# Cross-attention kernel: the two image chunks' picks in one matmul that opens the transposed scores, key turns behind the last weighted values, score turns behind a projection

## The chip, the cores and the metric

The kernel runs on one core of a Trainium2 chip. The metric is the device time of one execution in microseconds (us); the kernel before takes 1612.66 us, the median of three runs (1612.31 to 1616.88). Five engines work side by side, each through its own queue: TensorE (PE for matmuls, PEld for the loads of their weights), VectorE (DVE), ScalarE (ACT), GpSimd (POOL) and SyncE (SP, which issues DMAs). They wait for each other through semaphores.

## The reference

For each of 32 batches there are 112 tokens and a context of 375 rows (257 image rows, 118 text rows), 512 wide. The first layer is cross-attention with 16 heads of 32:

```
q = rms_norm(linear(layernorm(x), q_w, q_b), norm_q_w)
k, k_img = rms_norm(linear(ctx_txt, ...)), rms_norm(linear(ctx_img, ...))
out = softmax(q k_img^T / sqrt(32)) v_img + softmax(q k^T / sqrt(32)) v
x = x + linear(out, o_w, o_b)
```

The second layer picks 14 of the 112 tokens of each batch by a router score, runs a transformer block (causal attention over all 448 picked tokens, gated MLP) on them and adds the result to the layer norm of x, which is added to x.

## The kernel before, in words

The first 165 us project all queries. Then a loop goes over the batches: `body(i, n, m, p)` for batches 0 to 30 (i is this batch, n = i + 1 the one whose keys and values are projected meanwhile, m = i + 2, p = i - 1 the one that is finished), and `last` for batch 31. From 1240 us on comes the second layer. The order on every engine is written out by hand: each engine has its own `body`, and semaphores tie them.

PE's `body`, in its order. `scores(i, g)` for the four groups g of four heads gives scores by query, of which DVE takes each row's top (`group_max`). Between them stand projections: `values`, `output`, `keys`, each four to twelve matmuls of 512 columns in full shape (128 rows by 128 columns of weights). `turn_top` transposes the tops. `scores_T(i, g)` makes the scores again, by key, for four heads at once, one head in each 32-row strip of the array: three chunks of keys (119 text rows with an image row, and 128 and 128 image rows). In each chunk four matmuls multiply keys and queries in float32, which the trace shows as two records each, and four more (the picks, L1533) subtract the tops, in fp32r, one record each. The chunks lie side by side in a PSUM bank per head: columns 0 to 111, 112 to 223, 224 to 335. All four banks are read by ACT's `exps(i, g)` (L774 for the text chunk, L776 for both image chunks), and the next `scores_T` waits for that. `weighted_values(i, g, n)` (L1555) multiplies the probabilities by the values in 32-column strips, six sources of four matmuls (eight records) each; the last source is `prob_img`, for the image softmax's sum. POOL makes `prob_img` in `sum_image(i, g)` (L532) out of ACT's two image chunks, DVE adds the text chunk's image row to it in `add_tail(i, g)` (L1075), and only then can that last source start. DVE's `normalise(i, g)` (L1081, L1083, L1087) reads what comes out. `turn(n, k)` (L1477) transposes the three key tiles that DVE has scaled (`add_bias` L1049, `scale_k` L1055), and ACT's `split_kq` (L756 to L763) copies them out for the next batch's scores. It then copies a value tile (`value_image`, L785). `turn_score(p)` (L1515) transposes batch p's router score, whose ranks DVE counts.

POOL's `body` also splits the context (L495), takes roots (`inverse_rms`, L526), adds for the output (`output`, L536) and adds a bias row to the next residual (`residual`, L540, 112x512). ACT's and DVE's orders are not touched.

Of the kernel before, what the change touches and what calls it, by code (L numbers as in the profile page):

```python
# [12 lines left out]
B, L, D = 32, 112, 512  # L13
IMG, CTX = 257, 375
TXT = CTX - IMG
NH, HD = 16, 32
P = 128
KC = D // P
GH = P // HD
# [4 lines left out]
CHUNK_C = TXT + 1  # L24
# [7 lines left out]
CHUNKS = [(0, CHUNK_C), (CHUNK_C, P), (CHUNK_C + P, P)]  # L32
# [18 lines left out]
def build(nc, t, out):  # L51
    with ExitStack() as ctx:
# [3 lines left out]
        def sem(name):  # L56
            return ctx.enter_context(nc.semaphore(name))

        ps = ctx.enter_context(nc.psum_tensor("ps", [P, 8, 512], F32))
# [49 lines left out]
        pick_c = p1("pick_c", [P, NG, CHUNK_C], F32R)  # L109
        pick_img = p1("pick_img", [P, NG, P], F32R)  # L110
# [21 lines left out]
        k_all = p1("k_all", [P, KC, NKEY])  # L132
        q_hi = p1("q_hi", [P, NG, L], F32R)
        q_all = p1("q_all", [P, NG, L])
# [26 lines left out]
        topT = [p1(f"topT{e}", [P, L], F32R) for e in range(2)]  # L161
# [122 lines left out]
        st_full, exp_done, img_summed, tail_added = sem("st_full"), sem("exp_done"), sem("img_summed"), sem("tail_added")  # L284
# [206 lines left out]
        def _(pool):  # L491
# [36 lines left out]
            def sum_image(i, g):  # L528
                pool.wait_ge(exp_done, 8 * i + 2 * g + 2)
                if not isinstance(i, int) or i or g >= 2:  # L530
                    pool.wait_ge(pv_full, 4 * i + g - 1)
                nc.gpsimd.tensor_tensor(prob_img[:, g % 2], prob[:, g % 2, 1, :], prob[:, g % 2, 2, :], ALU.add).then_inc(img_summed, 1)  # L532
# [68 lines left out]
            def body(i, n, m, p):  # L601
                split_ctx(n)
                if p is not None:
                    normalise_h(p)
                inverse_rms(n, 1)
                if p is not None:
                    output(p)
                sum_image(i, 0)
                inverse_rms(n, 2)
                sum_image(i, 1)  # L610
                inverse_rms(n, 3)
                sum_image(i, 2)
                if p is None:
                    pool.wait_ge(rows_ready, 2)
                residual(i)
                sum_image(i, 3)

            def gather(c):
                nc.gpsimd.indirect_dma_start(xh_sel[:, c].rearrange("l a d -> l (a d)"), None, xh_dram[0:EARLY_B * L] if c < EARLY else xh_dram,
# [802 lines left out]
        def _(pe):  # L1422
# [89 lines left out]
            def turn_score(p):  # L1512

                pe.wait_ge(score_ready, p + 1)
                nc.tensor.transpose(ps[0:L, 7, 2 * L:3 * L], score_now[:].to_broadcast([L, L]), ident[0:L, 0:L]).then_inc(score_turned, 1)  # L1515

            def scores_T(i, g):
                if g == 0:
                    pe.wait_ge(s_done, 4 * i + 4)
                else:  # L1520
                    pe.wait_ge(exp_done, 8 * i + 2 * g)
                if g % 2 == 0:
                    pe.wait_ge(topT_ready, 2 * i + 1 + g // 2)
                for c, (at, rows) in enumerate(CHUNKS):
                    cols = slice(at, at + rows)
                    out_cols = slice(c * L, (c + 1) * L)
                    pick = pick_c if c == 0 else pick_img
                    for j in range(GH):
                        head = slice(HD * j, HD * (j + 1))
                        nc.tensor.matmul(ps[0:rows, 2 + j, out_cols], k_all[head, g, cols], q_all[head, g, :], start=True, stop=False)  # L1530
                    for j in range(GH):
                        head = slice(HD * j, HD * (j + 1))
                        last = nc.tensor.matmul(ps[0:rows, 2 + j, out_cols], pick[head, g, :], topT[g // 2][head, :], start=False, stop=True)  # L1533
                last.then_inc(st_full, 1)

            def weighted_values(i, g, n):
                pe.wait_ge(exp_done, 8 * i + 2 * g + 2)
                if g == 0:
                    pe.wait_ge(vtail_loaded, 16 * i + 16)
                    pe.wait_ge(b0_done, 4 * i + 4)  # L1540
                    pe.wait_ge(b1_done, value_slot(i, 1)[3] + 1)
                if g >= 2:
                    pe.wait_ge(pv_done, 4 * i + g - 1)
                bank = 6 + g % 2
                p_c, p_a, p_b = (prob[:, g % 2, c, :] for c in range(3))
                sources = ((0, ((v_last, p_c, CHUNK_C), (v_a, p_a, P), (v_b, p_b, P))), (1, ((v_txt, p_c, CHUNK_C),)),
                           (3, ((ones_txt, p_c, CHUNK_C),)), (2, ((ones_all, prob_img[:, g % 2], P),)))
                for slot, terms in sources:
                    for e, (left, right, rows) in enumerate(terms):
                        if slot == 2:  # L1550
                            pe.wait_ge(tail_added, 4 * i + g + 1)
                        for j in range(GH):
                            h = GH * g + j
                            cols = slice(HD * h, HD * (h + 1)) if slot < 2 else slice(0, HD)
                            last = nc.tensor.matmul(ps[HD * j:HD * (j + 1), bank, slot * L:(slot + 1) * L], left[0:rows, cols],  # L1555
                                                    right[0:rows, L * j:L * (j + 1)], start=e == 0, stop=e == len(terms) - 1)
                last.then_inc(pv_full, 1)
# [37 lines left out]
            def body(i, n, m, p):  # L1595
                scores(i, 0)
                values(i, 2)
                scores(i, 1)
                if p is not None:
                    output(p)  # L1600
                scores(i, 2)
                if p is not None:
                    pe.wait_ge(pv_done, 4 * i)
                turn_top(i, 0)
                keys(n, 0)
                scores(i, 3)
                keys(n, 1)
                turn_top(i, 1)
                scores_T(i, 0)
                keys(n, 2)  # L1610
                scores_T(i, 1)
                if p is not None:
                    pe.wait_ge(topT_ready, 2 * i + 2)
                    turn_score(p)
                weighted_values(i, 0, n)
                values(n, 0, range(0, 2))
                scores_T(i, 2)
                if p is not None:
                    pe.wait_ge(rank_done, i)
                weighted_values(i, 1, n)  # L1620
                scores_T(i, 3)
                values(n, 0, range(2, 4))
                weighted_values(i, 2, n)
                pe.wait_ge(exp_done, 8 * i + 8)
                for k in range(1, 4):
                    turn(n, k)
                weighted_values(i, 3, n)
                values(n, 1)

            hot = slot_hot[:].rearrange("l b k -> l (b k)")  # L1630
# [86 lines left out]
            for kc in range(KC):  # L1717
                made = nc.tensor.transpose(ps[:, kc // 2, L * (kc % 2):L * (kc % 2 + 1)], normed_last[:, kc * P:(kc + 1) * P], ident[0:L, 0:L])
# [174 lines left out]
```

## Time and profile before

| | us |
|---|---|
| median of three runs | 1612.66 |
| the profiled execution | 1612.68 |
| its span, first to last instruction | 1610.7 |
| PE busy | 1560.9 |
| PEld busy | 1213.2 |
| DVE busy | 1201.0 |
| ACT busy | 708.5 |
| POOL busy | 706.6 |

The loop over the batches has one pattern that repeats itself each 34.2 us. A timeline of one pass (here the one in which `scores_T(i, 0)` starts at 780.55 us) therefore stands for 31. In a timeline each row has the start, the duration, the engine, the line, the operation, what it writes and reads, and in brackets how long the engine stood idle before it and what ended that. Matmuls are pipelined: the distance from one start to the next is what a matmul costs, its duration is its latency.

### The profile page before, as it was taken

The numbers are of one execution on the slowest core, as the hardware profiler recorded it, in microseconds if no ns is written. First come the engines' busy times: TensorE is split into PE (matmuls) and PEld (weight loads), VectorE is DVE, ScalarE is ACT, GpSimd is POOL, SyncE is SP. The second block draws the span as 40 slices with busy tenths as digits, with TensorE's granted clock in tenths as the row PEclk, the third lists the DMA queues.
The fourth block names the chain that finished last, engine by engine and source line by source line (L and its number), as shares of the span: only waits on it lengthen the run. The fifth ranks groups of instructions, "written<-read, shape, count | busy, mean of one in ns | idle before, by whom it ended". The sixth has DMA issues, their size and how long they took to land.

```text
span 1610.7 us, 42276 instructions
## 1 busy us (share of the span) xinstructions
PE 1560.9 (97%) x16758; PEld 1213.2 (75%) x16758; DVE 1201.0 (75%) x1887; ACT 708.5 (44%) x1458; POOL 706.6 (44%) x785
## 2 busy tenths in 40 slices
PE   7999999999999999999999999999997999999997
PEld 5776777777777777777777777777776786777997
DVE  5753778877788878788788788787887586553986
ACT  5763444443444443444444444434444223555431
POOL 6762344334434344444344443344343592113752
PEclk9999999999999999999999999999997999999999
DMA  6842121112211112211112111122116324001000
GB/s 194 245 134 60 56 61 52 49 48 67 67 51 53 48 48 72 65 48 53 48 51 75 59 53 48 48 67 69 49 35 237 123 104 158 27 27 53 1 1 23
DMA packets 66167, 113.71 MB, mean 71 GB/s; under 512 B 21392, under 2 KB 36080, under 8 KB 64576
## 3 DMA queue, kind: packets, MB, share of 16 engines
q1 hardware_dynamic: 65280, 110.20, 21.5%
q0 software_dynamic: 832, 2.75, 0.6%
q8 instruction: 37, 0.61, 0.2%
q14 instruction: 18, 0.15, 0.0%
HBM read 82.59 MB, written 30.34 MB: 70 GB/s over the span
## 4 chain that ended last, share of the span: by engine, by line
PE 90%; ACT 5%; DVE 2%; POOL 1%; issue 1%; DMA 0%; ACTq 0%; POOLq 0%; DVEq 0%; SPq 0%
PE ps L1425 22%; PE ps L1426 19%; PE ps L1427 19%; PE ps L1555 8%; PE ps L1530 7%; PE ps L1503 3%; PE ps L1477 3%; PE ps L1759 2%; PE ps L1742 2%; ACT prob L776 2%; PE ps L1533 2%; PE ps L1751 1%; PE ps L1459 1%; ACT prob L774 1%; PE ps L1510 1%
## 5 line engine op out<-in xcount | busy, mean ns | idle before, releaser
L495 POOL TENSOR_TENSOR ctx_lo<-ctx_raw,ctx_hi 128x472 fp32r<-128x472 f32 x64 | 115.2, 1821 | 310.5 <-ACT ctx_hi L717 310.5
L532 POOL TENSOR_TENSOR prob_img<-prob 128x448 f32<-128x448 f32 x128 | 160.1, 1251 | 190.1 <-ACT prob L776 190.1
L1081 DVE RECIPROCAL rec<-ps 128x224 f32<-128x224 f32 x128 | 199.0, 1555 | 6.1 <-PE ps L1555 2.5
L774 ACT ACTIVATE prob<-ps 119x448 f32<-119x448 f32 x128 | 69.8, 545 | 210.6 <-PE ps L1533 210.6
L1530 PEld LDWEIGHTS ps<-q_all,k_all 32*128 32x128 f32 (+1 forms) x3072 | 121.9, 187 | 45.7 <-issue 31.8
L1070 DVE TENSOR_REDUCE top<-ps 112x4 f32<-112x1028 f32 x128 | 156.3, 1221 | 0.0
L1530 PE MATMUL ps<-q_all,k_all 32*128 32x112 f32 (+1 forms) x3072 | 148.3, 301 | 6.2 <-ACT prob L776 6.2
L750 ACT ACTIVATE sq_junk<-proj 128x513 bf16<-128x513 f32 (+1 forms) x96 | 61.2, 637 | 172.5 <-DVE proj L1049 172.5
L1069 DVE TENSOR_REDUCE top<-ps 112x4 f32<-112x472 f32 x128 | 83.0, 649 | 66.0 <-PE ps L1503 66.0
L1075 DVE SCALAR_TENSOR_TENSOR prob_img<-prob,ones_last,prob_img 23x448 f32<-23x448 f32 x128 | 90.3, 706 | 38.5 <-POOL prob_img L532 35.5
L776 ACT ACTIVATE prob<-ps 128x896 f32<-128x896 f32 x128 | 117.0, 914 | 0.0
L1425 PE MATMUL ps<-w_v_img_hi,ctx_hi 128*128 128x512 f32 x256 | 110.7, 433 | 0.0
L1425 PE MATMUL ps<-w_k_img_hi,ctx_hi 128*128 128x512 f32 x256 | 107.6, 420 | 0.0
L1427 PE MATMUL ps<-w_v_img_hi,ctx_lo 128*128 128x512 f32 x256 | 101.0, 395 | 0.0
L1426 PE MATMUL ps<-w_v_img_lo,ctx_hi 128*128 128x512 f32 x256 | 100.9, 394 | 0.0
L1427 PE MATMUL ps<-w_k_img_hi,ctx_lo 128*128 128x512 f32 x256 | 100.7, 393 | 0.0
L1426 PE MATMUL ps<-w_k_img_lo,ctx_hi 128*128 128x512 f32 x256 | 100.7, 393 | 0.0
L1049 DVE TENSOR_TENSOR proj<-ps,ki_bias 128x512 f32<-128x512 f32 x64 | 44.3, 693 | 50.6 <-PE ps L1427 50.6
L1427 PE MATMUL ps<-hT_hi,ring_lo 128*128 128x448 f32 x224 | 82.0, 366 | 0.0
L1533 PE MATMUL ps<-topT,pick_img 32*128 32x112 f32 x1024 | 81.3, 297 | 0.0
L526 POOL TENSOR_TENSOR rstd<-sq_sum,neg_half 128x1 f32<-128x1 f32 x96 | 52.7, 549 | 56.2 <-ACT sq_junk L750 56.2
L1338 DVE TENSOR_REDUCE neg_top<-ps 112x1 f32<-112x112 f32 (+1 forms) x64 | 28.5, 446 | 58.3 <-PE ps L1743 58.2
(333 smaller groups left out, 4416.7 us busy)
## 6 DMA issues: line engine op xcount, KB each, us to landing
ctx_raw<-in_ctx_dram SPq DMA_DIRECT2D x32, 748.0 KB, 4.2
xh_dram<-xh SPq DMA_DIRECT2D x32, 448.0 KB, 3.1
q_dram<-q_turned SPq DMA_DIRECT2D x28, 256.0 KB, 2.8
q_all<-q_dram SPq DMA_DIRECT2D x32, 224.0 KB, 3.0
xh<-in_x_dram SPq DMA_DIRECT2D x32, 224.0 KB, 2.8
out_dram<-out_sb SPq DMA_DIRECT2D x32, 224.0 KB, 2.3
xa<-in_x_dram SPq DMA_DIRECT2D x21, 256.0 KB, 3.4
ring<-in_wq_dram SPq DMA_DIRECT2D x1, 4096.0 KB, 13.9
```

The lines of the kernel that those rows point to most:

```text
L495: nc.gpsimd.tensor_tensor(ctx_lo[:, :, cols], ctx_raw[:, :, cols], ctx_hi[:, :, cols].bitcast(F32), ALU.subtract).then_inc(ctx_lo_done, 1)
L532: nc.gpsimd.tensor_tensor(prob_img[:, g % 2], prob[:, g % 2, 1, :], prob[:, g % 2, 2, :], ALU.add).then_inc(img_summed, 1)
L776: nc.scalar.activation(prob[:, g % 2, 1:3, :].rearrange("p c (j q) -> p j c q", j=GH), ps[:, 2:6, L:3 * L].rearrange("p j (c q) -> p j c q ...
L1070: nc.vector.tensor_reduce(rows[:, :, 2 * g + 1], ps[0:L, 2:6, TAIL:CTX], AX.X, ALU.max).then_inc(s_done, 1)
L1075: nc.vector.scalar_tensor_tensor(prob_img[last_rows, g % 2], prob[last_rows, g % 2, 0, :], ones_last[last_rows, 0:1], prob_img[last_rows, ...
L1081: nc.vector.reciprocal(rec[:], bank[:, 2:4]).then_inc(norm_step, 1)
L1425: nc.tensor.matmul(o_, a_hi, b_hi, start=start, stop=False)
L1426: nc.tensor.matmul(o_, a_hi, b_lo, start=False, stop=False)
L1427: return nc.tensor.matmul(o_, a_lo, b_hi, start=False, stop=stop)
L1530: nc.tensor.matmul(ps[0:rows, 2 + j, out_cols], k_all[head, g, cols], q_all[head, g, :], start=True, stop=False)
L1533: last = nc.tensor.matmul(ps[0:rows, 2 + j, out_cols], pick[head, g, :], topT[g // 2][head, :], start=False, stop=True)
L1555: last = nc.tensor.matmul(ps[HD * j:HD * (j + 1), bank, slot * L:(slot + 1) * L], left[0:rows, cols], right[0:rows, L * j:L * (j + 1)], st ...
```

## The change

On PE, `scores_T` now opens each chunk's sum with the pick instead of closing it, and the picks of the two image chunks, which have the same weights and the same moving operand, become one matmul of 224 columns that reads `topT` twice by a step of zero. In PE's `body`, `turn_score(p)` stands ahead of `scores_T(i, 1)` and so directly behind the projection `keys(n, 2)`; `weighted_values(i, 3, n)` stands ahead of the three key turns, directly behind `weighted_values(i, 2, n)`. Its own wait takes the place of the explicit one. On POOL, `sum_image(i, 3)` stands ahead of `residual(i)`. PE's `last` keeps its order; only its `scores_T` change.

```
--- before
+++ after
@@ POOL body
                 sum_image(i, 2)
+                sum_image(i, 3)
                 if p is None:
                     pool.wait_ge(rows_ready, 2)
                 residual(i)
-                sum_image(i, 3)
@@ scores_T
-                for c, (at, rows) in enumerate(CHUNKS):
-                    cols = slice(at, at + rows)
-                    out_cols = slice(c * L, (c + 1) * L)
-                    pick = pick_c if c == 0 else pick_img
+                def products(c, stop):
+                    at, rows = CHUNKS[c]
                     for j in range(GH):
                         head = slice(HD * j, HD * (j + 1))
-                        nc.tensor.matmul(ps[0:rows, 2 + j, out_cols], k_all[head, g, cols], q_all[head, g, :], start=True, stop=False)
-                    for j in range(GH):
-                        head = slice(HD * j, HD * (j + 1))
-                        last = nc.tensor.matmul(ps[0:rows, 2 + j, out_cols], pick[head, g, :], topT[g // 2][head, :], start=False, stop=True)
-                last.then_inc(st_full, 1)
+                        made = nc.tensor.matmul(ps[0:rows, 2 + j, c * L:(c + 1) * L], k_all[head, g, at:at + rows], q_all[head, g, :],
+                                                start=False, stop=stop)
+                    return made
+
+                for j in range(GH):
+                    head = slice(HD * j, HD * (j + 1))
+                    nc.tensor.matmul(ps[0:CHUNK_C, 2 + j, 0:L], pick_c[head, g, :], topT[g // 2][head, :], start=True, stop=False)
+                products(0, True)
+                for j in range(GH):
+                    head = slice(HD * j, HD * (j + 1))
+                    nc.tensor.matmul(ps[:, 2 + j, L:3 * L].rearrange("p (c q) -> p c q", c=2), pick_img[head, g, :],
+                                     topT[g // 2][head, :].unsqueeze(1).to_broadcast([HD, 2, L]), start=True, stop=False)
+                products(1, False)
+                products(2, True).then_inc(st_full, 1)
@@ PE body
                 keys(n, 2)
-                scores_T(i, 1)
                 if p is not None:
                     pe.wait_ge(topT_ready, 2 * i + 2)
                     turn_score(p)
+                scores_T(i, 1)
                 weighted_values(i, 0, n)
@@ PE body
                 weighted_values(i, 2, n)
-                pe.wait_ge(exp_done, 8 * i + 8)
+                weighted_values(i, 3, n)
                 for k in range(1, 4):
                     turn(n, k)
-                weighted_values(i, 3, n)
                 values(n, 1)
```

PE, one pass of the loop, from `scores_T(i, 1)` on, before. L1530 are products, L1533 picks, L1515 is the score turn, L1555 the first source of `weighted_values(i, 0, n)`:

```order
L1530 MATMUL ps<-q_all,k_all 119x112 x4
L1533 MATMUL ps<-topT,pick_c 119x112 x4
L1530 MATMUL ps<-q_all,k_all 128x112 x4
L1533 MATMUL ps<-topT,pick_img 128x112 x4
L1530 MATMUL ps<-q_all,k_all 128x112 x4
L1533 MATMUL ps<-topT,pick_img 128x112 x4
L1515 MATMUL ps<-ident,score_now 112x112
L1555 MATMUL ps<-prob,v_last 32x112 x4
```

The same place after; L1528 are products, L1534 and L1538 picks, L1562 `weighted_values`:

```order
L1515 MATMUL ps<-ident,score_now 112x112
L1534 MATMUL ps<-topT,pick_c 119x112 x4
L1528 MATMUL ps<-q_all,k_all 119x112 x4
L1538 MATMUL ps<-topT,pick_img 128x224 x4
L1528 MATMUL ps<-q_all,k_all 128x112 x8
L1562 MATMUL ps<-prob,v_last 32x112 x4
```

The score turn has moved ahead, the picks open the sums, and one four of picks of 112 columns is gone where another has become 224 wide.

PE at the end of the pass, from the last source of `weighted_values(i, 2, n)` to the first matmul of `values(n, 1)`, before; L1477 are the key turns:

```order
L1555 MATMUL ps<-prob_img,ones_all 32x112 x4
L1477 MATMUL ps<-ident,proj 128x118 x4
L1477 MATMUL ps<-ident,proj 128x128 x8
L1555 MATMUL ps<-prob,v_last 32x112 x4
L1555 MATMUL ps<-prob,v_a 32x112 x4
L1555 MATMUL ps<-prob,v_b 32x112 x4
L1555 MATMUL ps<-prob,v_txt 32x112 x4
L1555 MATMUL ps<-prob,ones_txt 32x112 x4
L1555 MATMUL ps<-prob_img,ones_all 32x112 x4
L1425 MATMUL ps<-w_v_img_hi,ctx_hi 128x512
```

and after:

```order
L1562 MATMUL ps<-prob_img,ones_all 32x112 x4
L1562 MATMUL ps<-prob,v_last 32x112 x4
L1562 MATMUL ps<-prob,v_a 32x112 x4
L1562 MATMUL ps<-prob,v_b 32x112 x4
L1562 MATMUL ps<-prob,v_txt 32x112 x4
L1562 MATMUL ps<-prob,ones_txt 32x112 x4
L1562 MATMUL ps<-prob_img,ones_all 32x112 x4
L1477 MATMUL ps<-ident,proj 128x118 x4
L1477 MATMUL ps<-ident,proj 128x128 x8
L1425 MATMUL ps<-w_v_img_hi,ctx_hi 128x512
```

The twelve turns have moved behind the six sources of the last group, which now has nothing between it and the group before.

POOL from the first sum of a pass to its last instruction, before; L532 is `sum_image`, L526 a root, L540 `residual`:

```order
L532 TENSOR_TENSOR prob_img<-prob 128x448
L526 TENSOR_TENSOR rstd<-sq_sum,neg_half 128x1
L532 TENSOR_TENSOR prob_img<-prob 128x448
L526 TENSOR_TENSOR rstd<-sq_sum,neg_half 128x1
L532 TENSOR_TENSOR prob_img<-prob 128x448
L540 TENSOR_TENSOR xh<-xh,out_bias 112x512
L532 TENSOR_TENSOR prob_img<-prob 128x448
```

and after:

```order
L532 TENSOR_TENSOR prob_img<-prob 128x448
L526 TENSOR_TENSOR rstd<-sq_sum,neg_half 128x1
L532 TENSOR_TENSOR prob_img<-prob 128x448
L526 TENSOR_TENSOR rstd<-sq_sum,neg_half 128x1
L532 TENSOR_TENSOR prob_img<-prob 128x448 x2
L540 TENSOR_TENSOR xh<-xh,out_bias 112x512
```

The residual's addition has moved from between the third and the fourth sum to directly behind the fourth.

## Rows read from the trace of the kernel before

**Rows 1.** The page: the span, and the chain that ended last.

```profile
span 1610.7 us, 42276 instructions
...
PE 90%; ACT 5%; DVE 2%; POOL 1%; issue 1%; DMA 0%; ACTq 0%; POOLq 0%; DVEq 0%; SPq 0%
```

**Rows 2.** Timeline, weight loads of `scores_T(i, 1)` and the score turn.

```profile
785.30 0.32 PEld L1530 LDWEIGHTS ps<-q_all,k_all 32*128 32x128 f32 x8
785.53 0.21 PEld L1533 LDWEIGHTS ps<-topT,pick_img 32*128 32x128 f32 x4
785.80 0.13 PEld L1515 LDWEIGHTS ps<-ident,score_now 112*112 112x112 f32 x1
```

**Rows 3.** Timeline, group 0's last source and the DVE instruction that it waits for.

```profile
786.16 0.68 DVE L1075 SCALAR_TENSOR_TENSOR prob_img<-prob,ones_last,prob_img 23x448 f32<-23x448 f32 x1
...
786.93 0.23 PEld L1555 LDWEIGHTS ps<-prob_img,ones_all 128*32 128x32 f32 x8
```

**Rows 4.** Timeline, PE from `weighted_values(i, 2, n)` to `values(n, 1)`.

```profile
794.31 0.16 PEld L1555 LDWEIGHTS ps<-prob,v_last 119*32 119x32 f32 x8 [0.36 <-ACT prob L776]
794.43 0.23 PEld L1555 LDWEIGHTS ps<-prob,v_a 128*32 128x32 f32 x8
...
795.20 0.23 PEld L1555 LDWEIGHTS ps<-prob_img,ones_all 128*32 128x32 f32 x8
795.60 1.26 PEld L1477 LDWEIGHTS ps<-ident,proj 118*128 118x128 f32 x12 [0.17 <-issue]
797.03 0.16 PEld L1555 LDWEIGHTS ps<-prob,v_last 119*32 119x32 f32 x8 [0.17 <-issue]
...
798.33 0.50 PE L1425 MATMUL ps<-w_v_img_hi,ctx_hi 128*128 128x512 f32 x1
798.66 0.39 PE L1426 MATMUL ps<-w_v_img_lo,ctx_hi 128*128 128x512 f32 x1
798.89 0.39 PE L1427 MATMUL ps<-w_v_img_hi,ctx_lo 128*128 128x512 f32 x1
```

**Rows 5.** Timeline, same pass: `scores_T(i, 3)`, POOL's sums and DVE's additions.

```profile
791.57 0.30 PEld L1530 LDWEIGHTS ps<-q_all,k_all 32*119 32x119 f32 x8 [0.40 <-ACT prob L776]
...
791.67 1.14 POOL L532 TENSOR_TENSOR prob_img<-prob 128x448 f32<-128x448 f32 x1 [2.68 <-ACT prob L776]
792.76 1.29 POOL L540 TENSOR_TENSOR xh<-xh,out_bias 112x512 f32<-112x512 f32 x1
794.33 1.57 POOL L532 TENSOR_TENSOR prob_img<-prob 128x448 f32<-128x448 f32 x1 [0.28 <-ACT prob L776]
...
794.21 0.68 DVE L1075 SCALAR_TENSOR_TENSOR prob_img<-prob,ones_last,prob_img 23x448 f32<-23x448 f32 x1
795.93 0.69 DVE L1075 SCALAR_TENSOR_TENSOR prob_img<-prob,ones_last,prob_img 23x448 f32<-23x448 f32 x1 [1.04 <-POOL prob_img L532]
```

**Rows 6.** Timeline, then single lines: count, duration ns min/median/max, first and last start.

```profile
781.43 1.28 POOL L536 TENSOR_TENSOR out_sb<-xh 112x512 f32<-112x512 f32 x1
...
781.49 1.76 DVE L1055 SCALAR_TENSOR_TENSOR proj<-proj,rstd,w_txt 118x512 f32<-118x512 f32 x1 [0.25 <-POOL rstd L526]
...
L1055 DVE SCALAR_TENSOR_TENSOR proj<-proj,rstd,w_txt x32: 744/1764/1767, 132.9 to 1192.0; 118x512 f32<-118x512 f32 x32
...
L1075 DVE SCALAR_TENSOR_TENSOR prob_img<-prob,ones_last,prob_img x128: 682/684/1700, 170.3 to 1243.2; 23x448 f32<-23x448 f32 x128
...
L1087 DVE TENSOR_TENSOR o_space<-o_two x128: 274/275/695, 173.5 to 1249.3; 128x112 f32<-128x112 f32 x128
```

**Rows 7.** Timeline, the last key copy on ACT and the next batch's first scores.

```profile
798.86 0.63 ACT L763 ACTIVATE k_all<-ps 128x512 f32<-128x512 f32 x1
...
801.30 0.43 PE L1503 MATMUL ps<-k_hi,q_hi 32*112 32x376 f32 x4
```

**Rows 8.** Windows in `last`: start:end, length, busy time by engine, PEclk, DMA.

```profile
1222.00:1223.00 1.00, 1.00 (x6) 0.95 (x6) 0.84 (x3) 1.00 (x2) 0.19 (x2) 0.50 0.00 0
1241.30:1243.30 2.00, 0.00 (x0) 0.00 (x0) 1.97 (x4) 2.00 (x5) 1.67 (x2) 1.00 0.98 410
```

## The prediction

> **What bounds the kernel now.** I read the page first: the chain that ended last is 90% PE [rows 1]. So the loop over the batches lasts as long as PE's queue, and a change there is worth what it takes from PE's starts, unless another engine is late at the same place. The question to put to the timeline is therefore how much air stands between PE and the engines that release it, place by place. I took one pass and looked at three things: what paces the transposed scores, what a change of the array's shape costs, and how late DVE, ACT and POOL are where PE needs them.
>
> In `scores_T` it is the weight loads that set the pace. The eight loads of one product (two fours, one head in each strip) take 785.53 - 785.30 = 0.23 us until the picks' four follow, 0.11 a four, and this goes on without a gap [rows 2]. Where PE goes from one shape to another, it runs dry and starts again: from the twelve turns to the strips of L1555 it takes 797.03 - 795.60 = 1.43, though the loads of the turns span only 1.26, and the first full matmul after the strips takes 798.66 - 798.33 = 0.33 where the next takes 0.23 [rows 4].
>
> Two places have hardly any air. For group 0, DVE's addition ends at 786.16 + 0.68 = 786.84 and PE takes up the source that needs it at 786.93 [rows 3]. For group 3, DVE's addition starts at 795.93, when POOL's sum ends (794.33 + 1.57 = 795.90), and ends at 796.62 [rows 5]; today the twelve turns hide that, since PE needs it only at 797.03 + 0.89 = 797.92 (the 0.89 is 795.20 - 794.31, five sources; four of them take 795.20 - 794.43 = 0.77, 0.19 each [rows 4]).
>
> **The change part by part,** as shifts against the same pass of the profile before.
>
> The merged picks. Each `scores_T` loses one four of loads, 0.11. It now ends on a product, and there the last loads stand 795.60 - 795.20 - 0.10 = 0.30 ahead of the next shape's, against 785.80 - 785.53 = 0.27 after a pick [rows 2, 4] (0.10 is half a source's 0.19, since its row has two fours of loads); 0.03 is given back. I take 0.08 each. The 224-column pick and its step of zero are in no row. If it streams at the pace of a 112-column one, it hides under the next load and the 0.08 stands; if the doubled width showed as two fours of today, nothing is gained; a loss I bound at another 0.08, if reading the same columns twice cost a load's time more. A gain over 0.11 is excluded, as no more than one four of loads goes.
>
> The score turn. Today it breaks the row strips from the column strips; behind `keys(n, 2)` it stands between matmuls of its own shape, so somewhat less than its slot goes. But that, and the 0.08 of `scores_T(i, 1)`, bring PE earlier to group 0's last source, where DVE isn't ready: its chain (bias, scaling, addition) hangs on the end of `keys(n, 2)` and not on what PE does since. Only `scores_T(i, 0)` stands ahead of that, so DVE's end moves 0.08, to 786.76. With 0.06 for the semaphore, between the 0.03 of DVE behind POOL (795.93 against 795.90 [rows 5]) and the 0.09 at this very place [rows 3], PE goes on at 786.82, not 786.93: a shift of -0.11 in all. How much the turn saves doesn't matter, it is turned into a wait of some 0.2.
>
> Groups 2 and 3. `scores_T(i, 3)` starts when ACT has read group 2 [rows 5]: it moves by 0.11 and by the 0.08 of `scores_T(i, 2)`, to 791.38. Its own 0.08 brings PE, and ACT's release of POOL, to -0.27: the fourth sum could start at 794.06.
>
> The reordered ending of PE's pass. Taking three breaks of shape to one: six sources straight behind six others take 1.17 (at 0.19 to 0.20), not 1.29 (795.60 - 794.31); twelve turns at 0.11 straight before values take 1.32 to 1.34, I take 1.34, not 1.43; the first value matmul 0.23, not 0.33. Together -0.31. With all of it, PE would be ready for group 3's last source at 795.20 + 1.17 - 0.27 = 796.10.
>
> What is late then is DVE, and here the POOL edit decides. Two of its effects are good: the residual leaves its old place, where it holds up L1087 (0.27 alone, 0.69 with it, once a pass) [rows 6]. So DVE's third addition moves from 794.21 by -0.08 - 0.41 to 793.72, and ends at 794.40; the fourth sum, which today ends 1.01 after that addition's end (795.90 against 794.89) [rows 5], then ends at 795.41. Now the residual starts 0.05 before that sum ends, as it does today behind the third (792.76 against 791.67 + 1.14 = 792.81) [rows 5], at 795.36. DVE's fourth addition can start only 0.03 after the sum, at 795.44, 0.08 behind the residual. The profile has that very geometry: L536, a POOL addition of the same 112x512, starts 0.06 ahead of DVE's L1055, and L1055 takes 1.76, the median of its 32, instead of 0.74, its least [rows 6]. And it has the very order: in `last`, POOL's residual already stands behind the fourth sum, and L1075 has its longest one there, 1.70 against a median of 0.68 (the last start is 1243.2) [rows 6]. So the fourth addition takes 1.70, to 797.14, and PE goes on at 797.20 instead of 796.10: a wait of 1.10 in each pass. POOL's instruction has the SBUF ports that both need, and DVE blocks until it ends.
>
> The Trainium skill says the same of this in "SBUF — State Buffer", section "SBUF: two separate sides": VectorE with two SBUF inputs and GpSimd take the shared ports by an exclusive lock, whoever starts first keeps them for the whole instruction. By that rule, the trace agrees, the wait is 1.1; without it, it would be under 0.1.
>
> From there: 0.40 to the turns, 1.34 for them, 0.23 to the second value matmul: 797.20 + 1.97 = 799.17, where it is 798.66 today. A pass gets longer by 0.51.
>
> Does the next pass take it up? The chain that ended last is nearly all PE's own work [rows 1], so there is hardly a wait that could shrink. Nor does it grow: ACT's last key copy ends at 799.49 today; it hangs on the turns, which move from 795.60 to 797.60, so it ends at 801.49 at the latest, ahead of the scores at 801.30 + 0.51 = 801.81 [rows 4, 7]. That leaves 0.3 of air; a later turn would be a wait of its own.
>
> 31 passes by 0.51 are 15.8; `last` gains 0.3 (four `scores_T`). The profiled execution took 1612.68, its span 1610.7, so 2 us lie outside, which the change doesn't touch; it stands at the median of the runs (1612.66). 1612.7 + 15.8 - 0.3 = 1628.
>
> Bounds of the unknown terms: with nothing from the merging, `scores_T` of groups 0, 2 and 3 each shift 0.08 less, 0.75 a pass, 1636; with a loss of 0.08, 1643. With 0.11 each and the semaphores 0.05 quicker, 0.36 a pass, 1624.
>
> **The rivals.**
>
> Faster: DVE gets the ports first, or the two don't meet. Then the fourth addition takes 0.69, ends at 796.13, PE waits 0.1 and the second value matmul comes at 796.19 + 1.97 = 798.16: -0.50 a pass, 1612.7 - 15.5 - 0.3 = 1597. For it speaks that DVE and POOL are within 0.08 of each other, and that another start order would do; against it, the median of L1055's 32 and the case in `last`. It decides once DVE starts ahead of the residual.
>
> No change: the two meet in part only, so that DVE loses 0.5 instead of 1.0, or the wait is shared with a longer gain on PE. 1612.7 plus or minus 5. No row shows a half blocked L1075.
>
> Slower, nearly as forecast but from the merging: the wide pick, the 1636 to 1643 above.
>
> Slower by far: the clock falls. PE's granted clock was 0.50 at 1222, after 1.8 us without a matmul, that is 1.2 instead of 2.4 GHz. Against it: 2.0 us without one from 1241.30 on passed at 1.00 [rows 8], and the new wait is only 1.1. If it fell for 3 us in each pass, 1.5 us a pass, 1628 + 46 = 1674. [...]
>
> **How the numbers follow.** The forecast with its near bounds (1619 to 1636) 0.70, the wide pick beyond 0.06, the clock 0.03, no change 0.07, the faster rival 0.14. The predicted time is 1628. The range leaves out the fast rival and the clock, and takes in most of no change and the wide pick: 1611 to 1641; the forecast's own is 1619 to 1636. A measurement of this kernel can tell 0.3% (5 us) from no change: slower by more 0.79, within it 0.07, faster 0.14.
>
> **What would show it.** Right: L1075 once a pass at 1.70 and L540 in the same stretch; a PE wait for DVE's `prob_img` of about 1.1 in 31 passes and one of about 0.2 in 30; L1087 always at 0.27; loads in `scores_T` at 0.11 with eight fours, not nine; a pass of 34.7 us. Wrong: L1075 at 0.68 throughout, with a pass of 33.7; or PE waiting at the key copies or at `scores_T(i, 1)`, where I see no wait; or 224-column picks with more than 0.11 to the next start.

## The result, and the profile after the change

The kernel after the change takes 1620.23 us (median of 9 runs, 1618.63 to 1623.29), the one before 1613.13 in the same runs (1610.59 to 1616.88). The ratio is 1.0041, 95% interval [1.0031, 1.0051]: slower by 7.1 us. The forecast was 1628, with a range of 1611 to 1641. The direction was right, the size was not: 15.3 us more were forecast, 7.1 came. Times of kernels are medians; of the four runs of `e8` below one took 4455 us, far off the other three, and is left out.

The page after, span and the chain that ended last (before: [rows 1]):

```profile
span 1619.2 us, 41249 instructions
...
PE 80%; ACT 8%; DVE 6%; POOL 4%; issue 2%; DMA 0%; POOLq 0%; ACTq 0%; DVEq 0%; SPq 0%
```

PE's part of the chain has gone from 90% to 80%: it now runs through ACT, POOL and DVE once in each pass. The list of waits (total us, times, longest) and the single lines (ns min/median/max, first and last start) say where:

```profile
PEld ps L1562 <- DVE prob_img L1075: 33.5, 35, 1.9
...
L1075 DVE SCALAR_TENSOR_TENSOR prob_img<-prob,ones_last,prob_img x128: 683/684/1697, 171.1 to 1252.6; 23x448 f32<-23x448 f32 x128
...
L1087 DVE TENSOR_TENSOR o_space<-o_two x128: 274/274/277, 174.3 to 1258.7; 128x112 f32<-128x112 f32 x128
```

PE waits some 30 times for about 1 us for DVE's addition, and L1087's 0.69 us are gone [rows 6]. The lengths of the full passes lie within 0.05 us of each other (34.45 to 34.50), so one pass tells the loop. The timeline of the pass that begins at 785.99 (start, duration, engine, line, operation; the same pass of before begins at 780.54):

```profile
785.99 0.18 PEld L1534 LDWEIGHTS ps<-topT,pick_c 32*119 32x119 f32 x4 [0.28 <-issue]
...
790.13 0.18 PEld L1534 LDWEIGHTS ps<-topT,pick_c 32*119 32x119 f32 x4 [0.28 <-issue]
790.23 0.29 PEld L1528 LDWEIGHTS ps<-q_all,k_all 32*119 32x119 f32 x8
790.43 0.20 PEld L1538 LDWEIGHTS ps<-topT,pick_img 32*128 32x128 f32 x4
790.54 0.53 PEld L1528 LDWEIGHTS ps<-q_all,k_all 32*128 32x128 f32 x16
791.18 0.16 PEld L1562 LDWEIGHTS ps<-prob,v_last 119*32 119x32 f32 x8
791.52 0.68 DVE L1075 SCALAR_TENSOR_TENSOR prob_img<-prob,ones_last,prob_img 23x448 f32<-23x448 f32 x1
792.26 0.16 PEld L1562 LDWEIGHTS ps<-prob_img,ones_all 128*32 128x32 f32 x8
792.59 0.19 PEld L1425 LDWEIGHTS ps<-w_v_img_hi,ctx_hi 128*128 128x128 f32 x1 [0.17 <-issue]
...
796.00 0.75 DVE L1055 SCALAR_TENSOR_TENSOR proj<-proj,rstd,w_img 128x512 f32<-128x512 f32 x1
796.22 0.38 PE L1562 MATMUL ps<-prob_img,ones_all 128*32 128x112 f32 x8
796.67 1.55 DVE L1081 RECIPROCAL rec<-ps 128x224 f32<-128x224 f32 x1
...
798.99 0.68 DVE L1075 SCALAR_TENSOR_TENSOR prob_img<-prob,ones_last,prob_img 23x448 f32<-23x448 f32 x1
799.50 1.17 POOL L532 TENSOR_TENSOR prob_img<-prob 128x448 f32<-128x448 f32 x1 [1.48 <-ACT prob L776]
800.63 1.27 POOL L540 TENSOR_TENSOR xh<-xh,out_bias 112x512 f32<-112x512 f32 x1
800.70 1.69 DVE L1075 SCALAR_TENSOR_TENSOR prob_img<-prob,ones_last,prob_img 23x448 f32<-23x448 f32 x1 [1.03 <-POOL prob_img L532]
802.44 0.16 PEld L1562 LDWEIGHTS ps<-prob_img,ones_all 128*32 128x32 f32 x8 [0.93 <-DVE prob_img L1075]
802.77 1.26 PEld L1477 LDWEIGHTS ps<-ident,proj 118*128 118x128 f32 x12 [0.17 <-issue]
804.35 0.39 PE L1426 MATMUL ps<-w_v_img_lo,ctx_hi 128*128 128x512 f32 x1
...
820.44 0.18 PEld L1534 LDWEIGHTS ps<-topT,pick_c 32*119 32x119 f32 x4 [0.28 <-issue]
```

This is to be seen: `scores_T` has one four of loads less (791.18 - 790.13 = 1.05, against 1.14 with nine fours before). The residual (L540) starts 0.07 ahead of DVE's fourth addition, and that addition takes 1.69, to 802.39, until the residual ends at 801.90 and some 0.5 more. PE has a gap of 0.93 in front of the last source. The pass takes 820.44 - 785.99 = 34.45 us, 34.46 in most, where it was 34.22 in most before: 0.23 to 0.24 more, and 31 passes by that are 7.1 to 7.4 us. (The spans of the two profiled executions differ by 8.5. Of this 7.7 stand in the 31 passes and 0.9 ahead of them, before the first `scores_T`; from `last` on the two take the same, 385.9 us. The first `scores_T` starts at 164.7 before, 165.6 after and at 163.8 in `e1`, though all three do the same up to there, so the 0.9 tells nothing of the change.)

### The profile page after: what moved, and what is told of

Read it like the earlier page. It is cut to its first block, busy times and chain, and to the rows that moved or that the text cites. A ratio compares the mean times of both kernels' runs of the same rounds, so it can differ in the third digit from the quotient of the medians.

```text
span 1619.2 us, 41249 instructions
## 1 busy us (share of the span) xinstructions
PE 1545.9 (95%) x16246; PEld 1193.4 (74%) x16246; DVE 1217.0 (75%) x1887; ACT 711.9 (44%) x1458; POOL 694.1 (43%) x785
## 4 chain that ended last, share of the span: by engine, by line
PE 80%; ACT 8%; DVE 6%; POOL 4%; issue 2%; DMA 0%; POOLq 0%; ACTq 0%; DVEq 0%; SPq 0%
PE ps L1425 20%; PE ps L1426 18%; PE ps L1427 18%; PE ps L1528 5%; DVE prob_img L1075 4%; PE ps L1562 3%; ACT prob L776 3%; PE ps L1503 3%; PE ps L1477 3%; POOL prob_img L532 3%; ACT prob L774 2%; PE ps L1534 2%; PE ps L1765 2%; PE ps L1748 2%; PE ps L1757 1%
## 5 line engine op out<-in xcount | busy, mean ns | idle before, releaser
L532 POOL TENSOR_TENSOR prob_img<-prob 128x448 f32<-128x448 f32 x128 | 147.9, 1156 | 221.1 <-ACT prob L776 221.1
L1075 DVE SCALAR_TENSOR_TENSOR prob_img<-prob,ones_last,prob_img 23x448 f32<-23x448 f32 x128 | 121.5, 950 | 39.9 <-POOL prob_img L532 36.8
L1528 PE MATMUL ps<-q_all,k_all 32*128 32x112 f32 (+1 forms) x3072 | 127.5, 277 | 0.0
L1528 PEld LDWEIGHTS ps<-q_all,k_all 32*128 32x128 f32 (+1 forms) x3072 | 107.3, 187 | 0.0
L1426 PE MATMUL ps<-w_v_img_lo,ctx_hi 128*128 128x512 f32 x256 | 100.6, 393 | 0.0
L1426 PE MATMUL ps<-w_k_img_lo,ctx_hi 128*128 128x512 f32 x256 | 100.6, 393 | 0.0
L762 ACT ACTIVATE k_hi<-ps 128x512 fp32r<-128x512 f32 (+1 forms) x96 | 57.9, 603 | 52.7 <-PE ps L1477 52.7
L526 POOL TENSOR_TENSOR rstd<-sq_sum,neg_half 128x1 f32<-128x1 f32 x96 | 52.8, 550 | 56.1 <-ACT sq_junk L750 56.1
L1562 PE MATMUL ps<-prob_img,ones_all 128*32 128x112 f32 x1024 | 49.9, 266 | 24.9 <-DVE prob_img L1075 24.9
```

What stands on the lines that cost most here:

```text
L1075: nc.vector.scalar_tensor_tensor(prob_img[last_rows, g % 2], prob[last_rows, g % 2, 0, :], ones_last[last_rows, 0:1], prob_img[last_rows, ...
L1426: nc.tensor.matmul(o_, a_hi, b_lo, start=False, stop=False)
L1528: made = nc.tensor.matmul(ps[0:rows, 2 + j, c * L:(c + 1) * L], k_all[head, g, at:at + rows], q_all[head, g, :], start=False, stop=stop)
```

## The experiments

Each ran beside the kernel before, on one chip for each group. Where kernels of two groups are compared, mind that the kernel before itself took 1612.91 to 1613.65 in them. The pass, and places in it, are read from each kernel's own trace as the median of its passes.

**Is it the residual's place against the fourth addition?** Four kernels went together; before was 1613.45.

`e1`: after, and the residual held back until the fourth addition has ended.

```diff
                 if p is None:
                     pool.wait_ge(rows_ready, 2)
+                pool.wait_ge(tail_added, 4 * i + 4)
                 residual(i)
```

> The changed kernel, but the residual's addition on POOL also waits until DVE has made its fourth addition (one more wait, no work less). Theory (ports): the residual behind the fourth sum costs the changed kernel its whole lead, as it blocks L1075 for 1.0 us a pass. Without the meeting L1075 takes 0.69 for group 3 as for the others, PE finds it ready (ready 15.45 us after the start of scores_T of group 0, wanted at 15.50), and the residual hides beside DVE's next reciprocal (1.55). A pass then takes 34.455 - 0.88 = 33.58 us, 31 passes save 27 against the changed kernel: 1593, that is 20 below the kernel before. Rival A (PE): the wide pick or the run of two groups of weighted values is what costs; then the wait changes nothing much, 1620 plus or minus 2. Rival B (timing of the fourth sum): DVE's addition is late as POOL's sum is late, with or without the residual behind it: 1615 to 1620.

Measured: 1593.46, ratio 0.9880 [0.9865, 0.9895], pass 33.56. In its timeline (the pass begins at 767.90, its lines stand one lower):

```profile
767.90 0.18 PEld L1535 LDWEIGHTS ps<-topT,pick_c 32*119 32x119 f32 x4 [0.28 <-issue]
...
781.41 1.18 POOL L532 TENSOR_TENSOR prob_img<-prob 128x448 f32<-128x448 f32 x1 [1.48 <-ACT prob L777]
783.47 1.27 POOL L540 TENSOR_TENSOR xh<-xh,out_bias 112x512 f32<-112x512 f32 x1 [0.89 <-DVE prob_img L1076]
...
782.62 0.69 DVE L1076 SCALAR_TENSOR_TENSOR prob_img<-prob,ones_last,prob_img 23x448 f32<-23x448 f32 x1 [1.04 <-POOL prob_img L532]
...
783.38 0.23 PEld L1563 LDWEIGHTS ps<-prob_img,ones_all 128*32 128x32 f32 x8
```

The fourth addition starts at the same place in the pass (14.72 after its begin, 14.71 in the changed kernel), takes 0.69, and PE's gap is gone. One wait on POOL takes 26.8 us off the changed kernel. With PE's edits in place, the collision is worth more than all that they bring.

`e2`: after with POOL's order of before, the residual between the third and the fourth sum.

```diff
                 sum_image(i, 2)
-                sum_image(i, 3)
                 if p is None:
                     pool.wait_ge(rows_ready, 2)
                 residual(i)
+                sum_image(i, 3)
```

> The changed kernel with POOL's order of before (third sum, residual, fourth sum). Theory (ports): the residual now blocks L1087 (0.68 instead of 0.27) and not L1075; DVE's fourth addition ends 0.25 to 0.27 earlier in the pass than before, and PE wants it some 0.35 before that. A pass takes about 33.9, the second matmul of values(n, 1) comes 0.35 earlier than before: 1602. Rival A (PE): no better than the changed kernel, 1618 to 1622.

Measured: 1603.23, 0.9935 [0.9922, 0.9949], pass 33.92. The third addition starts 13.44 into the pass and the fourth 15.18, both 0.45 later than in `e1`, since L1087 again has its long one, here 0.72; PE now waits some 0.4 for the fourth. So the POOL edit has a good half and a bad half: the residual is taken out of L1087's way, and put in the way of the fourth addition.

`e3`: before with the new `scores_T` alone.

> The kernel before with the new scores_T alone. If the merging gives 0.08 for each scores_T and groups 0, 2 and 3 count, with 0.07 more where a source that waited is left quicker, a pass is 0.34 shorter: 1602. If opening with the pick or the wide pick costs what the merging saves: 1613. If only the loads count and nothing waits for DVE in group 0, 0.085 x 4 x 31 = 10.5, much the same 1602; the profile tells which, by a wait for L1075 in group 0 of 0.05 to 0.1.

Measured: 1604.82, 0.9945 [0.9932, 0.9959], pass 33.93. `scores_T` takes 1.057 us instead of 1.136 in every group. That is the 0.08 forecast, and the pass is 0.29 shorter.

`e4`: before with the score turn alone moved ahead of `scores_T(i, 1)`.

> The kernel before with the score turn behind keys(n, 2) alone. Theory: it saves 0.12 of PE's queue, but DVE's addition for group 0 comes when it came, so PE waits there for L1075 for about 0.1 in 30 passes, and the pass gets 0.03 to 0.1 shorter: 1610 to 1612.5. Rival (PE's queue alone counts): 0.12 a pass, 1609.5 with no wait.

Measured: 1610.87, 0.9975 [0.9965, 0.9985], pass 34.11. The interest lies in its timeline (its pass begins at 779.45): DVE's first and second additions stand where they stood before, 5.61 and 9.37 into the pass, and yet the third comes at 13.57 instead of 13.67.

```profile
789.83 0.38 PE L1555 MATMUL ps<-prob_img,ones_all 128*32 128x112 f32 x8
...
790.28 1.56 DVE L1081 RECIPROCAL rec<-ps 128x224 f32<-128x224 f32 x1
793.00 0.68 DVE L1075 SCALAR_TENSOR_TENSOR prob_img<-prob,ones_last,prob_img 23x448 f32<-23x448 f32 x1
```

The reciprocal starts 0.07 behind PE's last matmul of group 1 (789.83 + 0.38 = 790.21), and the third addition follows it by 2.72 (2.73 before). Here it hangs on PE.

**What does each remaining edit do by itself, and does opening with the picks cost something?** Four more kernels; before was 1613.65.

`e5`: before with the twelve turns behind the last weighted values, and nothing else.

> The kernel before with the key turns behind the last weighted values alone; POOL's order is that of before. Theory: three breaks of shape become one, 0.31 a pass less for PE; but group 3's last source is wanted at 796.37 (time of the shown pass) and DVE's addition ends at 796.62 as before, so PE waits 0.3 and leaves that source 0.07 quicker: 0.08 a pass, 1611. PE then waits for L1075 in 31 passes, 0.25 to 0.3 each. Rival (PE's queue alone): 0.31 a pass, 1604.

Measured: 1610.01, 0.9976 [0.9967, 0.9985], pass 34.13.

```profile
793.57 0.16 PEld L1555 LDWEIGHTS ps<-prob_img,ones_all 128*32 128x32 f32 x8 [0.28 <-DVE prob_img L1075]
793.90 1.26 PEld L1477 LDWEIGHTS ps<-ident,proj 118*128 118x128 f32 x12 [0.17 <-issue]
```

The shape changes that it saves bring more than the 0.28 us that PE now waits, since the turns no longer cover DVE.

`e6`: before with POOL's new order alone.

> The kernel before with POOL's residual behind the fourth sum alone. Theory (ports): L1075 takes 1.70 for group 3 in each pass and ends near 797.2, but PE, with the twelve turns in between, wants it at 797.92 only: no PE wait, 1613 plus or minus 2. If the blocked addition costs time wherever it stands (DVE's reciprocals come later), 1620 and more.

Measured: 1614.21, 1.0002 [0.9993, 1.0011], pass 34.22: no change. But look at the rows:

```profile
793.88 1.28 POOL L540 TENSOR_TENSOR xh<-xh,out_bias 112x512 f32<-112x512 f32 x1
...
793.95 1.68 DVE L1075 SCALAR_TENSOR_TENSOR prob_img<-prob,ones_last,prob_img 23x448 f32<-23x448 f32 x1 [1.04 <-POOL prob_img L532]
...
796.35 0.23 PEld L1555 LDWEIGHTS ps<-prob_img,ones_all 128*32 128x32 f32 x8
```

The addition is blocked here too, for the full 1.68, and ends at 795.63; PE comes for it only at 796.35, behind the turns. The same edit costs some 17 us on top of the other three (1620.23 against `e2`'s 1603.23) and 0.6, which is nothing, by itself. The price is made by two edits together: one makes the addition late, the other takes away its cover.

`e7`: before with a `scores_T` in which the picks open, but three times 112 columns, not merged.

```diff
+                for c, (at, rows) in enumerate(CHUNKS):
+                    pick = pick_c if c == 0 else pick_img
+                    for j in range(GH):
+                        head = slice(HD * j, HD * (j + 1))
+                        nc.tensor.matmul(ps[0:rows, 2 + j, c * L:(c + 1) * L], pick[head, g, :], topT[g // 2][head, :], start=True, stop=False)
+                    last = products(c, True)
```

> The kernel before with scores_T opened by its picks, but the picks of the two image chunks left apart (nine fours of loads). If the merging is what gains in scores_T, this gives 0 to minus 0.03 for each, 1613 to 1616. If the opening is what gains, 1604 as the merged one.

Measured: 1619.07, 1.0031 [1.0020, 1.0042], pass 34.37. This was missed: I expected 1613 to 1616, and each `scores_T` takes 1.169 instead of 1.136.

```profile
787.22 0.18 PEld L1536 LDWEIGHTS ps<-topT,pick_c 32*119 32x119 f32 x4 [0.36 <-issue]
...
787.97 0.31 PEld L1528 LDWEIGHTS ps<-q_all,k_all 32*128 32x128 f32 x8
788.38 0.13 PEld L1515 LDWEIGHTS ps<-ident,score_now 112*112 112x112 f32 x1
```

So the 0.08 gained is two things: merging alone brings 1.169 - 1.057 = 0.112, a full four of loads, and with it unmerged the new order loses 0.033 (4 by 31 by 0.033 are 4.1 us; measured 5.4). The rows say where: the two fours of the last product stand 788.38 - 787.97 = 0.41 ahead of the next shape, so the last four 0.41 - 0.11 = 0.30, against 0.27 for a last four of picks [rows 2]; the eight fours ahead of it take 0.87 in both kernels. It is lost at the end, where the sum closes on a product.

`e8`: `e1`, and on DVE the first addition ahead of the scaling that stood before it.

```diff
                 add_bias(n, 3)
-                scale_k(n, 2)
                 add_tail(i, 0)
+                scale_k(n, 2)
```

> The changed kernel with the residual waiting for DVE's fourth addition, and on DVE group 0's addition ahead of the scaling of the second key tile (0.75 us). Theory: what still keeps PE waiting in group 0 is DVE's chain behind keys(n, 2). The addition then ends 0.75 earlier, PE's wait of some 0.2 goes, of which 0.07 comes back where the source is no longer left quicker: 0.12 a pass, 30 passes, 1590. Nothing is late next, as the scaled tile is wanted only by the key turns 9 us on. Rival: DVE's later work (the ranks, group 0's reciprocal) then stands in the way instead: 1593.

Measured: 1590.41, 0.9855 [0.9837, 0.9873], pass 33.47. DVE's first addition starts 4.87 into the pass instead of 5.53, and PE takes group 0's last source at 6.09 instead of 6.27 without a wait. The rest of the pass is of interest too (it begins at 767.70):

```profile
777.82 0.38 PE L1563 MATMUL ps<-prob_img,ones_all 128*32 128x112 f32 x8
...
778.38 1.55 DVE L1082 RECIPROCAL rec<-ps 128x224 f32<-128x224 f32 x1
```

PE ends group 1 at 778.20, 10.50 into the pass and 0.11 earlier than in `e1`, and yet the reciprocal stays at 10.68 and the third addition at 13.00. Here it no longer hangs on PE, but on DVE's own chain. So the fourth addition stays at 14.72 as well, and PE, which comes 0.11 earlier, has some 0.1 to wait for it.

**What exactly must be kept out of the way?** Three kernels; before was 1612.91.

`e9`: after, with a small write of 112x126 (`slot_hot` is free at this point) between the fourth sum and the residual, and no wait.

```diff
                 sum_image(i, 3)
+                nc.gpsimd.memset(slot_hot[:, 0:9], 0.0)
                 if p is None:
```

> The changed kernel with a small memset on POOL (126 columns of a buffer that is free in the loop, about 0.19 us) between the fourth sum and the residual; no wait is added. Theory (ports, whoever is first): DVE's fourth addition starts 0.03 after the sum's end, the residual now some 0.1 after it, so DVE goes through and the residual waits for it: L1075 0.68 to 0.85, L540 1.6 to 1.7, a pass of 33.57 to 33.7, 1593 to 1598. Rival (the POOL instruction behind the sum delays DVE whoever starts first): L1075 stays at 1.7 and more, 1620 to 1625.

Measured: 1594.85, 0.9888 [0.9868, 0.9908], pass 33.56.

```profile
851.57 0.20 POOL L614 MEMSET slot_hot<- 112x126 f32 x1
851.74 1.75 POOL L540 TENSOR_TENSOR xh<-xh,out_bias 112x512 f32<-112x512 f32 x1
...
851.67 0.69 DVE L1076 SCALAR_TENSOR_TENSOR prob_img<-prob,ones_last,prob_img 23x448 f32<-23x448 f32 x1 [1.04 <-POOL prob_img L532]
```

0.14 us decide over 25: in the changed kernel the residual starts 0.07 ahead of DVE and DVE takes 1.69; here it starts 0.07 behind and DVE takes 0.69, POOL's residual 1.75. This is the faster rival of the prediction (1597), put there by a write that nobody reads.

`e10`: `e1`, and a longer write (112x448) behind the fourth sum, so that it is under way when DVE starts.

```diff
                 sum_image(i, 3)
+                nc.gpsimd.memset(slot_hot[:], 0.0)
                 if p is None:
                     pool.wait_ge(rows_ready, 2)
+                pool.wait_ge(tail_added, 4 * i + 4)
```

> The kernel in which the residual waits for DVE's fourth addition, with a memset of 448 columns (POOL only writes; about 0.47 us) directly behind the fourth sum. If a POOL instruction that only writes SBUF doesn't stand in the way of an addition that reads two SBUF tensors: L1075 0.69, 1593.5 as without it. If any POOL instruction that is under way stands in its way: L1075 about 0.9 and PE's wait 0.2, some 4 to 6 more, 1598 to 1600.

Measured: 1592.53, 0.9875 [0.9853, 0.9898], pass 33.56.

```profile
851.43 0.47 POOL L614 MEMSET slot_hot<- 112x448 f32 x1
...
851.52 0.68 DVE L1077 SCALAR_TENSOR_TENSOR prob_img<-prob,ones_last,prob_img 23x448 f32<-23x448 f32 x1 [1.04 <-POOL prob_img L532]
```

DVE starts in the middle of it and takes its usual 0.68. What blocks is not POOL being busy: this write does not, the residual, which reads two tiles, does. A POOL instruction that reads one tile was not tried.

`e11`: `e8`, and in `scores_T` the image chunks first, opened by the wide pick; the text chunk comes last, its pick behind its product.

```diff
-                products(1, False)
-                products(2, True).then_inc(st_full, 1)
+                products(1, False, False)
+                products(2, False, True)
+                products(0, True, False)
+                for j in range(GH):
+                    head = slice(HD * j, HD * (j + 1))
+                    last = nc.tensor.matmul(ps[0:CHUNK_C, 2 + j, 0:L], pick_c[head, g, :], topT[g // 2][head, :], start=False, stop=True)
+                last.then_inc(st_full, 1)
```

> The kernel with the residual's wait and DVE's first addition ahead of the second scaling, and scores_T turned round: the two image chunks first, opened by their wide pick, then the text chunk, which its own pick closes. Picks-first with picks apart was 0.034 longer per scores_T than picks-last (1.169 against 1.135), so a sum that ends on a pick is left 0.034 earlier. If that is the end's doing: scores_T 1.02 instead of 1.057, 0.10 a pass, 1587.5. If it comes from the start with a pick: 1590.5 as without it.

Measured: 1588.11, 0.9851 [0.9827, 0.9874], pass 33.40. It is the lowest median of all, 24.8 us under the kernel before in the same runs; its interval overlaps that of `e8`.

```profile
770.38 0.19 PEld L1534 LDWEIGHTS ps<-topT,pick_img 32*128 32x128 f32 x4 [0.29 <-issue]
770.49 0.74 PEld L1529 LDWEIGHTS ps<-q_all,k_all 32*128 32x128 f32 x24
771.14 0.19 PEld L1541 LDWEIGHTS ps<-topT,pick_c 32*119 32x119 f32 x4
771.39 0.16 PEld L1563 LDWEIGHTS ps<-prob,v_last 119*32 119x32 f32 x8
...
781.69 0.16 PEld L1563 LDWEIGHTS ps<-prob_img,ones_all 128*32 128x32 f32 x8 [0.20 <-DVE prob_img L1076]
```

`scores_T` takes 1.01, as expected if the end decides: its last four, picks again, stands 771.39 - 771.14 = 0.25 ahead of the next shape, not 0.30. Four times 0.043 would be 0.17 a pass; 0.07 came, because PE waits for the fourth addition, by 0.20, and by 0.10 for the second. The additions move only by what PE gains up to the end of `keys(n, 2)`, 0.05, since from there on they follow DVE's own chain: that is the next bound.

## Why the prediction was right in its direction and wrong in its size

Offsets below count from the first load of `scores_T(i, 0)` (780.54 and 785.99 in the two passes shown) and are medians of the loop; the rows of one pass can be 0.01 or 0.02 off them. The value matmul that ends the prediction's sum (the first L1426) stood at 18.10 before. It was forecast 0.51 later, at 18.61, and came at 18.36. So 0.25 us a pass are missing, and 31 by 0.25 are 7.8 us, the whole of 1628 less 1620.2.

**The merged picks: right.** 1.136 to 1.057, -0.08 (all of them; shown alone by `e3`). The two parts were right as well: `e7` shows 0.11 for the merging and 0.03 given back at the end on a product.

**Group 0's last source: right, with one term missing.** DVE's first addition went from 5.61 to 5.53 and PE's source from 6.38 to 6.27, -0.11 as forecast. The source comes 792.26 - 791.89 = 0.37 after the one ahead of it, where 0.19 is usual: a wait of 0.18, forecast some 0.2. But PE then left it sooner. Behind a source that PE has waited for, the next start comes after 792.59 - 792.26 = 0.33 us, not the 0.40 that I carried over from sources taken without a wait [rows 4]. Everything behind moved by -0.18 instead of -0.11.

**DVE's third addition: this step failed.** The prediction said that it moves "from 794.21 by -0.08 - 0.41 to 793.72". It moved from 13.67 to 13.00, -0.67. The -0.41 of L1087 was right. The -0.08 was wrong: I had taken DVE's own chain from `keys(n, 2)` on as what it hangs on, as for the first addition. Between the two stands the reciprocal of group 1, and this waited for PE. The rows of before for it:

```profile
791.03 0.38 PE L1555 MATMUL ps<-prob_img,ones_all 128*32 128x112 f32 x8
...
790.63 0.75 DVE L1055 SCALAR_TENSOR_TENSOR proj<-proj,rstd,w_img 128x512 f32<-128x512 f32 x1
791.48 1.56 DVE L1081 RECIPROCAL rec<-ps 128x224 f32<-128x224 f32 x1
```

PE's group 1 ends at 791.41, and the reciprocal comes 0.07 behind it, 0.10 after L1055's end. After, PE's group 1 ends at 796.22 + 0.38 = 796.60, and the reciprocal again starts 0.07 behind. So the third addition moves by what PE moves there: 0.18 from group 0, and 0.08 of `scores_T(i, 2)`, 0.26 in all, and the -0.67 is 0.26 + 0.41. `e4` shows the dependence by itself: first and second additions unmoved, the third moved by 0.10 with PE. This makes 0.18 of the 0.25.

It could not have moved further. After, the reciprocal starts 0.08 ahead of the recorded end of L1055 (796.00 + 0.75 = 796.75), and so it does in `e8`, where PE has ended group 1 earlier and nothing but DVE's own chain is left to hold it. That chain did move by the 0.08 forecast; before, PE's end held the reciprocal 0.18 longer than the chain did, and the change took away just this 0.18. The prediction looked for DVE's chain and passed over the wait that stood in it.

**The fourth sum and the blocked addition: right.** The fourth addition started 1.72 behind the third (forecast 1.72; it is 1.72 to 1.73 in every kernel here), 0.07 behind the residual (forecast 0.08), and took 1.69 (forecast 1.70). `e1`, `e2` and `e9` take the collision away in three ways, and each time the addition takes 0.69. With the third addition 0.18 earlier the fourth is so too, and PE's wait was 0.93 instead of 1.10. What keeps the 1.72 constant is a second collision, the other way round: POOL's fourth sum starts while DVE makes its third addition and is held by it. It takes 1.57 before, 1.17 after and 1.47 in `e11`, where the third sum takes 1.13 to 1.14, and each time it ends 1.00 behind the end of that addition.

**The ending: right, with the same missing term.** From the waited-for source to the turns PE took 802.77 - 802.44 = 0.33, forecast 0.40; from the turns to the second value matmul 1.58, forecast 1.57. This is the other 0.07: 0.18 + 0.07 make the 0.25.

**The next pass takes up nothing: right.** Pass and second value matmul moved by nearly the same, 0.24 and 0.26. `scores(i + 1, 0)` started without a wait for the key copies. The clock didn't fall (the page gives the same tenths of PEclk, all 9, in the loop), and the wide pick cost nothing that shows: its four loads are followed by the next after 790.54 - 790.43 = 0.11.

**`last`: forecast 0.3 less, and none came.** From its first `scores_T` to the end both kernels take 385.9 us. In both, three of DVE's four additions in `last` are held (1.54 to 1.70 each), if not the same three, and part of it runs at the lower granted clock (0.50 [rows 8]). What of this ate the 0.3 no run shows; it is 0.3 of the whole and not what made the forecast miss.

The working of the forecast went wrong where it took one engine's chain for free of the other at a place where both had moved. Both errors had one sign, and times 31 they were the 7.8 us.

## What to carry to other kernels

An instruction moved off one collision can be moved into the next: an order on POOL is judged against what DVE starts within the next 0.1 us, and a wait for DVE's instruction, or a short write between the two, can be worth more than the whole change (26.8 and 25.4 us here, against the changed kernel). An edit that costs nothing by itself (`e6`) is priced together with the edit that removes its cover. When the shifts of a step are summed, write beside each instruction the last thing that released it, for every engine anew: before the change DVE's first addition hung on its own chain and its third on PE; after it the third hung on both at once, and 0.11 more from PE (`e8`) moved it by nothing.

## What the runs showed of the hardware that I had not expected

- The first start decides, but not to the hundredth of the record. With POOL's residual 0.07 ahead, DVE's addition took 1.69; with it 0.07 behind, 0.69. But in `last` the record has DVE ahead of a POOL sum by 0.02 in the kernel before and by 0.05 in the one after, and it was DVE whose addition took longer, 1.64 and 1.66 instead of 0.68, while the sums took their usual time. In the passes of `e3` DVE is ahead of the fourth sum by 0.06, takes 0.68, and the sum takes 1.62. So a lead of 0.05 in the record is too little to tell who holds. The rows of `last`, before and then after:

```profile
1241.62 1.64 DVE L1075 SCALAR_TENSOR_TENSOR prob_img<-prob,ones_last,prob_img 23x448 f32<-23x448 f32 x1
1241.63 1.14 POOL L532 TENSOR_TENSOR prob_img<-prob 128x448 f32<-128x448 f32 x1 [1.02 <-ACT prob L776]
...
1245.62 1.66 DVE L1075 SCALAR_TENSOR_TENSOR prob_img<-prob,ones_last,prob_img 23x448 f32<-23x448 f32 x1
1245.67 1.13 POOL L532 TENSOR_TENSOR prob_img<-prob 128x448 f32<-128x448 f32 x1 [3.52 <-ACT prob L776]
```

- The one that is held does not end with the holder. DVE's fourth addition ends 0.48 to 0.49 behind the residual, POOL's sum 1.00 behind DVE's addition.

- A POOL write of 0.47 us with nothing to read left DVE's two-input addition at 0.68 us (`e10`).
- A source for which PE has waited is left after 0.33 us, one that it takes in the flow after 0.40.
- A pick of 224 columns, with a step of zero over the same 112, took no more time in the stream of loads than one of 112: 0.11 us to the next four in both.
- A `scores_T` that ends on a product is left 0.03 to 0.05 us later than one that ends on picks: its last four of loads stands 0.30 ahead of the next shape (`e7`, the changed kernel), against 0.27 before and 0.25 in `e11`. What in the engine makes the difference no run shows.
